# A five-pass graph kernel: 19 of 25 row ends are transposed on VectorE in blocks of 32 x 32

## What is computed

```python
h = adj @ (adj.T @ e); out = layernorm(h) * gamma + beta + res     # layer 0, e from h by small weights
out = adj @ h                                                      # layer 1
T1 = adj @ h; T2 = 2 * adj @ T1 - h; T3 = 2 * adj @ T2 - T1        # layer 2
out = h @ w0 + T1 @ w1 + T2 @ w2 + T3 @ w3 + bias
out = relu(dis * ((adj + I) @ (dis * (h @ W + b))))                # layer 3, dis = degree ** -0.5
```

## Time and profile before

| | us |
|---|---|
| median of 3 runs (1479.26 to 1480.37) | 1480.0 |
| the profiled execution, its own time | 1481.6 |
| its span in the trace | 1479.7 |
| TensorE busy | 1455.0 |
| VectorE busy | 397.4 |
| ScalarE busy | 243.2 |
| DMA, mean over the span | 353 GB/s |

### The profile page before, as it was taken

The page is one execution under the profiler, slowest core; times in us unless marked ns, Lnnn a source line. Parts: engine busy times, 40 slices in busy tenths (PEclk is TensorE's granted clock), DMA queues, the critical chain, the costliest instruction groups (busy, mean ns, idle before and its releaser), DMA issues.

```text
span 1479.7 us, 17938 instructions
## 1 busy us (share of the span) xinstructions
PE 1455.0 (98%) x7901; PEld 631.4 (43%) x7901; DVE 397.4 (27%) x412; ACT 243.2 (16%) x481; POOL 84.2 (6%) x67
## 2 busy tenths in 40 slices
PE   6999999999999999999999999999999999999998
PEld 3565565565556653333333333333333333333332
DVE  6585445445445424110110100000000011101121
ACT  2343343343334352000000100000000000000000
POOL 2300000000000028000000000000000000000000
PEclk9999999999999999999999999999999999999999
DMA  9999999999999998999996787899787948996897
GB/s 328 389 397 388 399 401 392 394 390 398 382 402 367 381 397 345 420 421 419 421 417 213 306 341 282 341 345 319 295 313 266 310 162 336 348 374 239 341 421 312
DMA packets 97457, 522.18 MB, mean 353 GB/s; under 512 B 18748, under 2 KB 18788, under 8 KB 54628
## 3 DMA queue, kind: packets, MB, share of 16 engines
q1 hardware_dynamic: 90292, 519.35, 90.3%
q10 hardware_dynamic: 7088, 1.67, 0.5%
HBM read 414.83 MB, written 106.17 MB: 352 GB/s over the span
## 4 chain that ended last, share of the span: by engine, by line
PE 61%; DMA 3%; DVE 0%; ACT 0%; issue 0%
PE turned L577 34%; PE acc L577 23%; DMA staged<-adj_t 2%; DMA over_last<-adj_t 1%; PE t_acc L743 1%; PE turned L611 1%; PE turned L769 1%; PE t_rows L753 0%; PE turned L775 0%; PE t_acc L659 0%; PE t_rows L659 0%; DVE staged L1114 0%; DVE staged L1126 0%; DVE h_acc L1006 0%; DVE staged L1112 0%; DVE staged L1117 0%
## 5 line engine op out<-in xcount | busy, mean ns | idle before, releaser
L963 DVE TENSOR_REDUCE deg_part<-raw 128x4 f32<-128x3072 f32 (+1 forms) x70 | 220.5, 3192 | 0.0
L815 ACT ACTIVATE staged<-turned 128x512 f32<-128x512 f32 x331 | 168.6, 619 | 242.1 <-PE turned L611 241.6
L611 PEld LDWEIGHTS turned<-ident,raw 128*128 128x128 f32 x1600 | 174.2, 140 | 24.9 <-issue 24.9
L611 PE MATMUL turned<-ident,raw 128*128 128x128 f32 x1600 | 184.7, 274 | 0.0
L588 PE MATMUL t_acc<-raw,E 128*64 128x384 f32 (+1 forms) x1120 | 181.8, 475 | 0.7 <-DMA raw<-in_adj_dram 0.7
L577 PE MATMUL acc<-staged,t_cur 128*64 128x512 f32 x720 | 161.1, 596 | 0.0
L577 PE MATMUL turned<-over_last,C 128*64 128x512 f32 x664 | 150.4, 593 | 0.0
L577 PE MATMUL turned<-over_last,R 128*64 128x512 f32 x616 | 139.9, 594 | 0.3 <-DMA over_last<-adj_t 0.3
L588 PEld LDWEIGHTS t_acc<-raw,E 128*64 128x64 f32 x1120 | 79.4, 138 | 100.6 <-issue 91.3
L1152 POOL TENSOR_TENSOR rstd<-rstd,minus_half 128x8 f32<-128x8 f32 (+1 forms) x30 | 44.2, 1473 | 1289.8 <-DVE rstd L954 1289.8
L577 PE MATMUL acc<-over_last,C 128*64 128x512 f32 x416 | 93.9, 593 | 0.0
(11 more groups left out here) (133 smaller groups left out, 877.0 us busy)
## 6 DMA issues: line engine op xcount, KB each, us to landing
over_last<-adj_t SPq DMA_DIRECT2D x177, 1024.0 KB, 8.2
staged<-adj_t SPq DMA_DIRECT2D x93, 1024.0 KB, 9.2
raw<-in_adj_dram SPq DMA_DIRECT2D x60, 1536.0 KB, 19.0
adj_t<-staged SPq DMA_DIRECT2D x30, 3072.0 KB, 16.6
over_wide<-adj_t SPq DMA_DIRECT2D x24, 1024.0 KB, 9.1
raw<-in_adj_dram SPq DMA_DIRECT2D x10, 1024.0 KB, 13.9
adj_t<-over_last SPq DMA_DIRECT2D x8, 1024.0 KB, 9.6
adj_t<-C SPq DMA_DIRECT2D x2, 1024.0 KB, 20.5
```

What stands on the lines that cost most here:

```text
L611: last = nc.tensor.transpose(turned[q % TURN_BANKS][:, a * P:(a + 1) * P], raw_of(g, u // 2 * 2 + b)[:, sub, c * P:(c + 1) * P], ident[:, :])
L815: nc.scalar.activation(turned_into(g, u)[:, i * B:(i + 1) * B], turned[q % TURN_BANKS][:, :], ACT.Copy) \
L963: nc.vector.tensor_reduce(deg_part[:, of(m), g], raw_of(g, m), AX.X, ALU.add).then_inc(deg_summed, 1)
```

## The change

For all rows of passes 0, 1 and 2 and the first four of pass 4, 19 of 25, TensorE's four transposes at the row end fall away. VectorE, right behind the save to `y_sb`, transposes sixteen times a block row of 32 partitions x 4 blocks of 32 x 32 and writes it to another 32 partitions of a new buffer `z_sb` in SBUF (two of them, in room that other buffers left). What read `t_acc` reads `z_sb` then. The rows of pass 3 and the very last row stay as they are. The plan gets more distance: `READY` of pass 0 goes from 9 to 11, of passes 1 and 2 from 3 to 4, and `WEIGH` of pass 0 from 5 to 7. The numbers of tiles, loads and duals stay.

```diff
+SQ = 32
...
-NORM, MAKE, WEIGH = 3, 4, 5
-READY = [9, 3, 3, 8, None]
+NORM, MAKE = 3, 4
+WEIGH = {0: 7, 3: 5}
+READY = [11, 4, 4, 8, None]
...
-        y_node = t_acc[:, :].rearrange("p (a d) -> p a d", d=D)
+        z_at = (LATE_SLOTS * TILE_WORDS + 2 * B, LATE_SLOTS * TILE_WORDS + 3 * B)
+        z_sb = [staged[:, z:z + B] for z in z_at]
...
+        BY_TENSOR = [r for r, (p, m) in enumerate(plan.rows) if p == 3 or r + 1 == len(plan.rows)]
+        BY_VECTOR = [r for r in range(len(plan.rows)) if r not in BY_TENSOR]
+
+        def y_node(r):
+
+            rows = y_rows_bank[:, :] if r in BY_TENSOR else z_sb[r % 2]
+            return rows.rearrange("p (a d) -> p a d", d=D)
...
-                for r in plan.row_at(s, 1, *range(PASSES)):
+                for r in [r for r in plan.row_at(s, 1, *range(PASSES)) if r in BY_TENSOR]:
                     pe.wait_ge(y_saved, r + 1)
-                    if r >= 1:
-                        p, m = plan.rows[r - 1]
-                        if p == 2:
-                            pe.wait_ge(rows_ready, features_no(3, m))
-                        else:
-                            pe.wait_ge(y_read, Y_READ_NO[r - 1])
+                    if r > BY_TENSOR[0]:
+                        pe.wait_ge(y_read, Y_READ_NO[BY_TENSOR[BY_TENSOR.index(r) - 1]])
                     for a in range(SUB):
                         last = nc.tensor.transpose(y_rows_bank[:, a * P:(a + 1) * P], y_sb[r % 2][:, a * P:(a + 1) * P],
                                                    ident[:, :])
                     last.then_inc(y_rows, 1)
-                for r in plan.row_at(s, WEIGH, *WEIGHED):
+                for r in [r for p in WEIGHED for r in plan.row_at(s, WEIGH[p], p)]:
...
+            def turn_squares(r):
+
+                src = y_sb[r % 2].rearrange("p (a b n) -> p a b n", b=4, n=SQ)
+                dst = z_sb[r % 2].rearrange("p (a h e c) -> p a h e c", h=2, e=2, c=SQ)
+                for h in range(2):
+                    for e in range(2):
+                        q = 2 * h + e
+                        for b in range(4):
+                            last = nc.vector.transpose(dst[b * SQ:(b + 1) * SQ, :, h, e, :],
+                                                       src[q * SQ:(q + 1) * SQ, :, b, :])
+                last.then_inc(y_squares, 1)
...
                 for r in plan.row_at(s, 2, *range(PASSES)):
                     p, m = plan.rows[r]
                     x = X[:, of_pair(m), :]
-                    dve.wait_ge(y_rows, r + 1)
+                    if r in BY_TENSOR:
+                        dve.wait_ge(y_rows, BY_TENSOR.index(r) + 1)
+                    else:
+                        dve.wait_ge(y_squares, BY_VECTOR.index(r) + 1)
+                    node = y_node(r)
...
                     dve.wait_ge(multiplied, plan.own_no[plan.last_own[p, m]])
-                    if r >= 2:
-                        dve.wait_ge(y_rows, r - 1)
+                    if r - 2 in BY_TENSOR:
+                        dve.wait_ge(y_rows, BY_TENSOR.index(r - 2) + 1)
...
                     ins.then_inc(y_saved, 1)
+                    if r in BY_VECTOR:
+                        dve.wait_ge(y_saved, r + 1)
+                        turn_squares(r)
```

More of the change, by code:

```diff
@@ L324, in gnn_stack @@
         y_rows = sem("y_rows")
+        y_squares = sem("y_squares")
         y_read = sem("y_read")
@@ L756, in _ @@
                 for batch in range(2):
-                    for r in plan.row_at(s, WEIGH + 1 + batch, 0):
+                    for r in plan.row_at(s, WEIGH[0] + 1 + batch, 0):
                         q = plan.weigh_no[r]
@@ L771, in _ @@
                         last.then_inc(feat_mult, 1)
-                for r in plan.row_at(s, WEIGH + 1, 3):
+                for r in plan.row_at(s, WEIGH[3] + 1, 3):
                     pe.wait_ge(feat_copied, plan.weigh_no[r] + 1)
@@ L1095, in _ @@
                     x = X[:, of_pair(m), :]
-                    dve.wait_ge(y_rows, r + 1)
+                    if r in BY_TENSOR:
[3 more added lines that the diff above has]
+                    node = y_node(r)
                     if p in WEIGHED:
-                        nc.vector.tensor_tensor(x, y_node, x, ALU.add).then_inc(y_read, 1)
+                        nc.vector.tensor_tensor(x, node, x, ALU.add).then_inc(y_read, 1)
                         dve.wait_ge(y_read, Y_READ_NO[r])
@@ L1103, in _ @@
                         dve.wait_ge(weigh_saved, 4 * ROWS)
-                        stt(c, y_node, 2.0, c, ALU.mult, ALU.add).then_inc(rows_ready, 1)
-                        stt(x, y_node, -2.0, x, ALU.mult, ALU.add).then_inc(y_read, 1)
+                        stt(c, node, 2.0, c, ALU.mult, ALU.add).then_inc(rows_ready, 1)
+                        stt(x, node, -2.0, x, ALU.mult, ALU.add).then_inc(y_read, 1)
                         dve.wait_ge(y_read, Y_READ_NO[r])
@@ L1108, in _ @@
                         c = C1[:, of_pair(m), :]
-                        stt(c, y_node, 2.0, c, ALU.mult, ALU.add).then_inc(rows_ready, 1)
+                        stt(c, node, 2.0, c, ALU.mult, ALU.add).then_inc(rows_ready, 1)
                     else:
                         o = cen[r % 2][:, :, :]
-                        nc.vector.tensor_tensor(o, y_node, R[:, of_pair(m), :], ALU.add).then_inc(y_read, 1)
+                        nc.vector.tensor_tensor(o, node, R[:, of_pair(m), :], ALU.add).then_inc(y_read, 1)
                         dve.wait_ge(y_read, Y_READ_NO[r])
```

## The result

| | before | changed |
|---|---|---|
| median of the runs, us | 1479.7 (4 runs) | 1470.6 (4 runs) |
| lowest and highest, us | 1479.26, 1480.37 | 1469.67, 1473.46 |
| profiled execution: own time and span, us | 1481.6, 1479.7 | 1471.1, 1469.1 |

The ratio is 0.9939, 95% interval [0.9927, 0.9951]: 9.1 us faster by the medians, 7.3 to 10.8 by the interval. Measured again later, beside other kernels, it was 1470.5 against 1480.1, ratio 0.9932 [0.9918, 0.9946].

What follows compares the result with a forecast made beforehand. TensorE bounds the middle, DMA both ends. Passes 0 to 2 give 14 x 0.73 - 0.4 = 9.8 us, pass 4 nothing, no stall: 1481.6 becomes 1471.8 profiled, median forecast 1470.2 us, range 1468.5 to 1477.5.

Steps and rivals of the forecast that it cites:

- The price of a row end, 0.73 us: TensorE at a row end: four transposes cost 0.73 us including switching, so 19 removed groups are worth 13.9 us at most.
- No seam is left: TensorE's row ends in passes 0 to 2: without transposes, products follow 1.72 us apart.
- rival E: TensorE's row ends keep their seam through semaphore waits of the same length: 1478 to 1481 us, chance 0.05.
- One transpose at 0.29 us, 4.6 us for sixteen: VectorE's added work per row, priced from its 128-element copies; bounds 0.20 and 0.69 us each.
- The room for it: Time for the sixteen before TensorE's first reader: up to 5.08 us in passes 1 and 2, 4.9 in pass 0.
- no stall is charged: TensorE's wait for row results: VectorE's 4.6 us is hidden, with 0.3 to 0.4 us to spare.
- rival B: VectorE's transposes take 0.31 to 0.40 us each and stick out; at 0.36, 1475.3 us; chance 0.18.
- Early end: Pass 0, DMA-bound start: row 0's 0.73 us is lost, plus 0.4 us at a later load.
- Late end: Pass 4, bound by DMA: its four row ends, 2.9 us, turn into load waits and gain nothing.
- Rival D: Last stretch not bound by DMA: all but the first row end count, 12.7 us gained, 1467.3; chance 0.05.
- Rival C: VectorE's blocks take twice the time per element, 0.42 us each: 11.9 us sticks out, 1482 us; chance 0.10.
- cover gone, each us beyond 5 costs up to seven: TensorE's waits for VectorE: once the sixteen exceed 5 us, each us more costs up to seven in all.

Runs made afterwards that it cites:

- The distances alone: Kernel before with READY 11, 4, 4 and WEIGH 7 of the change, all 25 row ends on TensorE: 1480.5 against 1480.3, ratio 1.000.
- the run with READY 3: The changed kernel with READY of passes 1 and 2 back from 4 to 3: 1479.0 against 1481.0 for the kernel before, ratio 0.999.
- with 10.1 us: The changed kernel with the sixteen transposes done twice, 10.1 us per row: 1536.4 against 1481.0 for the kernel before, ratio 1.038.
- the other loop order: The changed kernel with the loops over the sixteen turned round, four in a row writing one group of 32 partitions: 1469.9 in one execution.

## Why the prediction was right

- **The price of a row end, 0.73 us.** Right: passes 1 and 2, with ten row ends and nothing else in the way, gained 7.3 us in the trace. The distances alone gained nothing, so it is the removed work.
- **No seam is left.** Right, as the timeline shows; rival E (the seam stays) is out.
- **One transpose at 0.29 us, 4.6 us for sixteen.** The one term that was mis-sized: 0.315 and 5.04. The record of one is 0.303, not 0.29, and another 0.013 lies between two, since each is held until the last is finished. The estimate from the 311 ns that the Trainium skill gives for bf16 ("VectorE: DVE Perf Modes", section "The three transpose paths"), 5.0 us, was nearer than the row I took, and the 0.2 us that it put at stake were lost: at the last row of pass 0 product 137 came 2.65 us behind its neighbour instead of 2.45.
- **The room for it.** I had 5.08 us in passes 1 and 2; the run with READY 3 gives 5.03, and the sixteen take 5.05. TensorE starts there no sooner than VectorE lets it, and loses about 0.02 us a row to it. So of the 0.4 us that I believed to be spare nothing is left, and "no stall is charged" held by luck: the mis-sized term stopped just where the waiting starts. At 0.36 each it would have been rival B.
- **Early end.** I lost row 0's 0.73 and 0.4 us at one wait. In the changed kernel's trace rows 1 to 4 of pass 0 brought 2.4 us between products 44 and 137, against 4 x 0.73 - 0.4 = 2.5: the loads took 0.34 us from product 51 (forecast 0.4) and the norm the 0.2 us at product 137. Whether row 0's share is wholly lost is open: the end of product 44 came between 647.7 and 648.8 us in the four traces with pass 0's row ends on TensorE, and between 646.5 and 648.4 in nine with them on VectorE, and the start of pass 0 itself moved by up to 2.2 us from trace to trace.
- **Late end.** Right in the main: the last pass on TensorE again is no slower, alone on VectorE it brings nothing the rounds can tell, and the waits for loads grew from 0.9 to 3.5 us (3.8 forecast). Rival D (the last pass counts as well) is out. But the waits are no fixed number: 2.5 us in the second trace of the change, and alone on VectorE the last pass brought back only 1.8 of its 2.9 us as waits. That these row ends are worth nothing is not shown, only that they are worth less than 2 us. Pass 3's rows, which lie ahead of the chain of loads, do count.
- **Rival C**, the sixteen sticking out, did not come (its sum of 11.9 us is 11.8 by its own terms), but "cover gone, each us beyond 5 costs up to seven" was too kind: with 10.1 us, it cost 66 us, 13 per us beyond 5: ten rows waited and not seven, and the clock came down too.

## What to carry to other kernels

Moving work from a full engine to an idle one pays by the number of places where the time is not set by something else: find those first (here a queue of loads at both ends), and don't spend the move on them. Price the move by start-to-start times around it, not by the record of the moved operation (0.73 us for 0.66), and the new work by the pace at which its instructions start when each has to wait for the last. And measure the room for the new latency by taking a step of distance away: with no margin left the time looks just as it would with 4 us of it.

## What the runs showed of the hardware

- VectorE's 32-partition transposes of f32 with 128 elements per partition take 0.303 us each and start 0.315 apart where the group of 32 partitions read or written changes (the change and the other loop order); where four in a row stay in one group they take 0.26 and start down to 0.193 apart.
- Around the end of each of eight idle times of TensorE of 4.7 to 5.2 us the granted clock fell to 0.50 for 3.4 or 6.8 us, which reached into the work behind. At two of 3.5 us and five of 1.5 to 1.6 us it did not fall, but it did, for 3.4 us, behind one of 1.78 us (all of pass 3 on VectorE): the length of the idle time alone does not tell. At the five rows of passes 1 and 2, waits of 4.9 us made the products behind them come 6.6 to 8.0 us later.
- At the end of the change, while output rows were being stored, products that waited each for its load of 1 MB started 2.57 to 2.59 us apart; in pass 0 they ended 2.48 to 2.49 us apart. Whether the stores make the difference was not tried.
